# Second expert layer with W2 stationary and 512 tokens moving, with the relu's result multiplied by the choice on GpSimd

## The chip, the cores and the metric

The kernel runs on one core of a Trainium2 chip. The metric is the device time of one execution, in microseconds. The core has five engines that run side by side and hand work over by semaphores: TensorE (PE, matmuls, results in the PSUM banks), VectorE (DVE), ScalarE (ACT), GpSimd (POOL) and SyncE (SP), which issues most of the DMAs. Each engine takes its instructions strictly in the order of its own list.

## The reference

Two attentions and a mixture of experts over x of shape (2, 1024, 128), all in float32.

```
x = layernorm(x + attention_1(x))                 # 8 heads of 16, causal
x = x + attention_2(rmsnorm(x) * norm1_w)         # 16 heads of 8, through a latent of 64, causal
h = rmsnorm(x) * norm2_w
top = argmax(h @ gate_w.T + gate_b)               # one of 4 experts for each token
y_e = relu(h @ W1[e].T + b1[e]) @ W2[e].T + b2[e] # 128 -> 512 -> 128, all 4 experts
x = layernorm(x + sum_e onehot(top)[e] * y_e)
```

Every expert is computed for every token, and the choice (0 or 1) selects one of the four results.

## The kernel before

Tokens are split into batches b (0, 1) and blocks i (0, 1) of 512 tokens, each four tiles of 128. The attentions are worked off in 12 groups of four heads: groups 0 to 3 are the first attention, 4 to 7 the second attention of batch 0, 8 to 11 that of batch 1. A group needs its row maxima first (matmuls in `maxima`, L1137 to L1148, reduced on DVE by L1552), then scores (L1169), the exponential on ACT (L1338), on diagonal steps a mask on POOL (`mask`, L1044), the product with the values (`weigh`, L1186), a copy out of PSUM (L1343) and a transpose (`turn`, L1197).

Between these the program places the smaller stages. `ready(b, i)` makes the input of the experts: feed, y, residual (L1582), square, the inverse root in 13 short DVE steps on [128, 4] (`inverse_root`, L1474 to L1490), hat and x12 on POOL (L1095, L1101), feed and feat once more, gate (L1251) and `pick` (L1519 to L1527), which makes `onehot`. `experts(b, i)` is the stage that is changed. It has 16 chunks c of 128 hidden units, four to an expert e:

- `hidden` (L1318): one matmul with a chunk of W1 stationary and the block's 512 tokens of `feat` moving, into a bank of its own.
- `relu` (L1400): ACT reads that bank, adds b1 and writes `hid`, which holds two experts' chunks.
- `expert` (L1255 to L1264): when all four chunks of expert e are there, for each of the four token tiles t one small bf16 matmul for b2 (L1260) and four matmuls (L1262) with the tile's 128 tokens of `hid` stationary and 128 columns of W2 moving. A float32 matmul stands in the trace as two matmul instructions, so a tile has eight rows of L1262.
- `pick_up` (L1649): four DVE instructions an expert, each `xn = psum * onehot[e] + xn` for 128 tokens.

After the last expert of a block come the moments, the inverse root, the layer norm and the store.

The order of all instructions is made ahead of time by `order`: each step has a wanted position in units of groups (`EXPERTS`, `READY`, ...), a cost in `COSTS` and a list of steps it needs, and the planner always takes the step with the smallest sum of expected stall and position. `EXPERTS` puts the blocks of batch 0 at 7.9 to 11.4, so beside the attention of groups 8 to 11, and those of batch 1 at 11.6 to 14, mostly behind the last group, which ends with group 12. Banks for the small stages come from a pool: while the attention runs, only banks 2 and 3 (`SIDE`) are in it; after the step `quiet`, all eight. A bank is given out again when the reader named in `READER` has read it; `expert` holds one bank for one expert, from its first tile to its `pick_up`.

## Time and profile before

| | |
|---|---|
| median of three runs | 650.6 us |
| lowest and highest | 646.08 and 653.72 us |
| the profiled execution | 650.81 us |
| its span, first to last instruction | 649.1 us |
| busy: PE, DVE, ACT, POOL | 569.2, 427.3, 337.1, 157.4 us |
| mean granted TensorE clock | 0.95 |

The span is 1.7 us shorter than the time of the same execution. Groups 8 to 10 take about 393 to 535 us, with the experts of batch 0 beside them (hidden from 386.5 on); group 11 ends with its copy at 579.3 us, and from there to 640.4 us only the expert stages of batch 1 are left. The rest is the last block's norm and store. "Busy" for PE is the union of instructions whose ends are modelled, so full stretches mean that PE always had something under way.

### The profile page before, as it was taken

To read this page: it belongs to the slowest core of one execution; us is meant where nothing else is said; L and a number is where in the kernel's file an instruction comes from. 1 tells how busy PE (TensorE), PEld (TensorE's weight loads), DVE (VectorE), ACT (ScalarE), POOL (GpSimd) and SP (SyncE) were. 2 spreads that over 40 slices of the span, in tenths; PEclk is the share of its full clock that TensorE was granted. 3 is DMA by queue.
4 is the path that set the end of the run, shared out by engine and by line. 5 is a ranking of instruction groups with operands and counts; after the bars stand their busy time and mean duration, and the time that the engine had idled before them with its cause. 6 is when DMAs were issued, how large, how long until landed. Compare 5 with 4: busy or idle time off the path is not lost.

```text
span 649.1 us, 10791 instructions
## 1 busy us (share of the span) xinstructions
PE 569.2 (88%) x3917; PEld 262.7 (40%) x3933; DVE 427.3 (66%) x1091; ACT 337.1 (52%) x641; POOL 157.4 (24%) x213
## 2 busy tenths in 40 slices
PE   6678399878699978888999999999999998899994
PEld 3333133433233333332333344555534544357662
DVE  4589288889978785886888786856686614314313
ACT  4313165646446645754776767455575566652330
POOL 9611021325523243523121221301201102201000
PEclk9879599989889996996999999999999999899998
DMA  4966203001011002011010101001000000000000
GB/s 126 208 158 225 63 2 95 5 25 48 29 43 44 15 5 71 26 46 56 2 50 3 51 2 50 1 4 50 1 18 1 2 3 17 0 1 1 18 0 16
DMA packets 27845, 25.63 MB, mean 39 GB/s; under 512 B 7377, under 2 KB 24401, under 8 KB 27538
## 3 DMA queue, kind: packets, MB, share of 16 engines
q1 hardware_dynamic: 27410, 24.17, 13.2%
q0 software_dynamic: 384, 0.79, 0.6%
q8 instruction: 31, 0.51, 0.3%
q14 instruction: 20, 0.16, 0.1%
HBM read 17.30 MB, written 7.34 MB: 38 GB/s over the span
## 4 chain that ended last, share of the span: by engine, by line
PE 67%; DVE 9%; SPq 9%; ACT 7%; DMA 4%; issue 3%; POOL 1%; DVEq 0%; ACTq 0%
PE ps L1186 15%; PE ps L1169 11%; PE ps L1262 11%; PE ps L1318 9%; PE ps L1148 8%; ACT pr L1338 6%; SPq L889 4%; PE ps L1251 3%; PE ps L1245 2%; DVE mparts L1552 2%; PE ps L1197 2%; PE ps L1260 2%; DMA scr0k<-parts 2%; PE ps L1226 1%; PE ps L1143 1%
## 5 line engine op out<-in xcount | busy, mean ns | idle before, releaser
L1338 ACT ACTIVATE pr<-ps 128x512 f32<-128x512 f32 (+1 forms) x480 | 249.2, 555 | 194.9 <-PE ps L1169 157.3
L1552 DVE TENSOR_REDUCE mparts<-ps 128x1 f32<-128x512 f32 (+3 forms) x480 | 277.2, 629 | 91.3 <-PE ps L1148 90.1
L1148 PE MATMUL ps<-ks,qs 61*128 61x512 bf16 (+7 forms) x576 | 147.7, 341 | 17.5 <-DMA qs<-nparts 12.6
L1169 PE MATMUL ps<-qs,ks 64*128 64x512 bf16 (+7 forms) x560 | 141.6, 337 | 19.8 <-ACT pr L1338 10.3
L1186 PE MATMUL ps<-pr,vs 128*32 128x512 f32 (+3 forms) x1152 | 125.9, 509 | 6.8 <-ACT pr L1338 4.7
L1044 POOL TENSOR_SCALAR_AFFINE_SELECT pr<-pr 128x512 f32<-128x512 f32 x96 | 61.3, 639 | 282.1 <-ACT pr L1338 281.9
L1169 PEld LDWEIGHTS ps<-qs,ks 64*128 64x128 bf16 (+1 forms) x576 | 41.8, 95 | 139.7 <-ACT pr L1338 88.5
L1262 PE MATMUL ps<-w,work 128*128 128x128 f32 x512 | 74.1, 288 | 0.0
L1318 PE MATMUL ps<-feat,w 128*128 128x512 f32 x128 | 66.3, 622 | 0.1
L1148 PEld LDWEIGHTS ps<-ks,qs 61*128 61x128 bf16 (+1 forms) x576 | 49.3, 98 | 37.1 <-DVE mparts L1552 18.6
L1262 PEld LDWEIGHTS ps<-w,work 128*128 128x128 f32 x512 | 61.9, 191 | 4.3
L1400 ACT ACTIVATE work<-ps,b 128x512 f32<-128x512 f32 x64 | 43.8, 687 | 37.3 <-PE ps L1318 36.7
L1649 DVE SCALAR_TENSOR_TENSOR xn<-ps,onehot,xn 128x128 f32<-128x128 f32 x48 | 13.5, 343 | 42.1 <-PE ps L1262 42.1
L1186 PEld LDWEIGHTS ps<-pr,vs 128*32 128x32 f32 x1152 | 23.2, 108 | 44.4 <-issue 22.0
L1137 PE MATMUL ps<-cmask,identb 128*128 128x128 bf16 (+1 forms) x96 | 24.5, 256 | 7.7 <-DMA ks<-scr0k 4.0
L1318 PEld LDWEIGHTS ps<-feat,w 128*128 128x128 f32 x128 | 20.6, 189 | 19.8 <-issue 15.6
L1143 PE MATMUL ps<-cmask,identb 64*128 64x128 bf16 (+1 forms) x96 | 23.4, 244 | 0.9 <-DVE mparts L1552 0.6
L1143 PE MATMUL ps<-cmaskx,identx 64*128 64x128 bf16 (+1 forms) x96 | 23.4, 244 | 0.5 <-DVE mparts L1552 0.4
L1137 PEld LDWEIGHTS ps<-cmask,identb 128*128 128x128 bf16 x96 | 9.6, 101 | 29.1 <-DVE mparts L1552 20.6
L1145 PE MATMUL ps<-cmaskx,identx 64*128 64x64 bf16 (+1 forms) x96 | 19.3, 201 | 0.0
L1145 PE MATMUL ps<-cmask,identb 64*128 64x64 bf16 (+1 forms) x96 | 19.2, 200 | 0.0
L1343 ACT COPY ot<-ps 128x512 f32<-128x512 f32 x24 | 14.1, 587 | 7.5 <-PE ps L1186 7.5
(136 smaller groups left out, 499.6 us busy)
## 6 DMA issues: line engine op xcount, KB each, us to landing
qs<-scr0q SPq DMA_DIRECT2D x48, 64.0 KB, 4.0
qs<-scr1q SPq DMA_DIRECT2D x84, 32.0 KB
ks<-scr1k SPq DMA_DIRECT2D x84, 32.0 KB
ks<-scr0k SPq DMA_DIRECT2D x36, 64.0 KB, 2.2
scr0q<-parts SPq DMA_DIRECT2D x4, 384.0 KB, 3.0
scr0k<-parts SPq DMA_DIRECT2D x4, 384.0 KB, 4.3
scr1q<-parts SPq DMA_DIRECT2D x4, 384.0 KB, 2.5
scr1k<-parts SPq DMA_DIRECT2D x4, 384.0 KB, 2.5
```

Source lines behind the costliest of these rows:

```text
L1044: pool.affine_select(out=p, in_=p, compare_op=ALU.is_ge, fill=0.0, base=0, pattern=[[0, HG], [1, P]], channel_multiplier=-1).then_inc(done ...
L1137: pe.matmul(bank[:, :, w - P:w], identb[:, :], cmask[:, 0:nh, :], start=True, stop=False, skip_group_check=True)
L1143: pe.matmul(bank[:, :, w - P:w], low[0][own, :], low[1][own, 0:nh, :], start=True, stop=False, skip_group_check=True)
L1145: pe.matmul(bank[:, :, w - HALF:w], high[0][own, :], high[1][own, 0:nh, HALF:P], start=False, stop=False, skip_group_check=True)
L1148: last = pe.matmul(bank[:, h, :], queries(F, 0, h0 + h, i * P, P), keys(F, 0, h0 + h, 512 * c, w), start=not diagonal, stop=True, skip_gro ...
L1169: last = pe.matmul(to[:, h, :], keys(F, 3, h0 + h, j * P, P), queries(F, 3, h0 + h, qb * 512 + lo, n), start=True, stop=True)
L1186: last = pe.matmul(ps[VW * h:VW * (h + 1), PVB, lo:lo + n], vs[:, F % VSLOTS, j, VW * h:VW * (h + 1)], pr[:, st % PSLOTS, h, 0:n], start=( ...
L1262: last = pe.matmul(to, hid[:, e % 2, c, t * P:(t + 1) * P], w2[:, e * HC + c, :], start=False, stop=(c == HC - 1), skip_group_check=True)
L1318: pe.matmul(side(*step), w1[:, c * P:(c + 1) * P], feat[:, columns(b, i)], start=True, stop=True).then_inc(done["hidden"], 1)
L1338: act.activation(pr[:, st % PSLOTS, h0:h0 + nh, 0:STEPS[st][3]], scores_at(F, v), ACT.Exp, scale=GROUPS[F][0].scale).then_inc(exped, 1)
L1400: act.activation(hid[:, c // HC % 2, c % HC, :], side("hidden", b, i, c), ACT.Relu, bias=b1[:, c:c + 1]).then_inc(done["relu"], 1)
L1552: dve.tensor_reduce(mparts[:, F % SLOTS, h0:h0 + nh, i, c], maxes_at(F, u), AX_X, ALU.max).then_inc(taken, 1)
```

## The change

The second layer is turned round. `expert(b, i, c)` now works by chunk: W2's chunk is stationary, the 512 tokens of `hid` move, and all 16 chunks of a block are summed in one bank. So that the sum over experts is the mixture, each chunk of `hid` is multiplied in place by 0 or 1 before (`picked`, on GpSimd). The factor is needed with tokens along the free dimension and the same in all partitions. `choice_turn` (PE) and `choice_copy` (ACT) turn the choice round, `spread` (PE) and `spread_copy` (ACT) repeat one expert's row in 128 partitions, four times a block, into `masks`. b2 is added by one matmul with the choice moving. The sum, 128 features by 512 tokens, is copied out by ACT (`mix`), turned back by four transposes (`mix_turn`), and one DVE addition (`pick_up`) adds it to the residual. `masks`, `chosen` and `yT` lie in memory that earlier stages have left. The bank of the sum is held from a block's chunk 0 to its `mix`.

The plan's own figures are 0.9 for an `expert` chunk, 1.2 for `picked`, 0.35 for `choice_turn`, 0.23 for `spread`, 0.6 for the three copies, 0.58 for `mix_turn` and 0.7 for `pick_up`; positions in `EXPERTS` stay.

```diff
 def experts(b, i):
 
-    out = []
-    for c in range(E * HC + 2):
-        if c < E * HC:
-            out += [("hidden", b, i, c), ("relu", b, i, c)]
-        if c % HC == 1 and c > HC:
-            e = c // HC - 1
-            out += [("expert", b, i, e, t) for t in range(4)] + [("pick_up", b, i, e)]
-    return out + [("moments", 2, b, i)] + root("result", b, (i,)) + [("layer_norm", 2, b, i), ("out", b, i)]
+    chunks = range(E * HC)
+    return ([("choice_turn", b, i), ("choice_copy", b, i)]
+            + [(kind, b, i, e) for e in range(E) for kind in ("spread", "spread_copy")]
+            + [(kind, b, i, c) for c in chunks for kind in ("hidden", "relu", "picked", "expert")]
+            + [("mix", b, i), ("mix_turn", b, i), ("pick_up", b, i), ("moments", 2, b, i)]
+            + root("result", b, (i,)) + [("layer_norm", 2, b, i), ("out", b, i)])
 
 
 READER = {"feed": "feat", "y": "residual", "latent": "lat_copy", "lat_turn": "lat_feat", "v_proj": "v_out",
-          "gate": "pick", "hidden": "relu", "expert": "pick_up"}
+          "gate": "pick", "choice_turn": "choice_copy", "spread": "spread_copy", "hidden": "relu", "expert": "mix",
+          "mix_turn": "pick_up"}
 
...
-    if kind == "relu":
-        b, i, c = a
-        turn = 4 * (2 * b + i) + c // HC - 2
-        return [("hidden", *a)] + [("expert", turn // 8, turn // 4 % 2, turn % 4, 3)] * (turn >= 0)
-    if kind == "expert":
-        return [("relu", *a[:2], a[2] * HC + HC - 1), ("b2_parts",)]
+    if kind in ("relu", "picked", "expert"):
+        own = {"relu": "hidden", "picked": "relu", "expert": "picked"}[kind]
+        before = E * HC * (2 * a[0] + a[1]) + a[2] - 2 * HC
+        return ([(own, *a)] + [("spread_copy", *a[:2], a[2] // HC)] * (kind == "picked")
+                + [("expert", before // (2 * E * HC), before // (E * HC) % 2, before % (E * HC))] * (kind == "relu" and before >= 0)
+                + [("choice_copy", *a[:2]), ("b2_parts",)] * (kind == "expert"))
+    if kind == "choice_turn":
+        return [("pick", *a), ("lo", 15)]
+    if kind == "choice_copy":
+        return [("choice_turn", *a)]
+    if kind == "spread":
+        return [("choice_copy", *a[:2])]
+    if kind == "spread_copy":
+        return [("spread", *a)] + [("picked", 0, a[1], a[2] * HC + HC - 1)] * (a[0] == 1)
+    if kind == "mix":
+        return [("expert", *a, E * HC - 1)] + [("mix_turn", 0, a[1])] * (a[0] == 1)
+    if kind == "mix_turn":
+        return [("mix", *a)]
     if kind == "pick_up":
-        return [("expert", *a, 3), ("pick", *a[:2]), ("x12", *a[:2])]
+        return [("mix_turn", *a), ("x12", *a)]
...
-                    bank_reader[bank] = (READER[kind],) + step[1:4]
+                    bank_reader[bank] = (READER[kind],) + (step[1:3] if kind == "expert" else step[1:4])
...
-        b2p = sb("b2p", [3, E * C], BF16)
-        ones3 = sb("ones3", [3, P], BF16)
+        b2p = sb("b2p", [PARTS * E, C], BF16)
+        own_row = sb("own_row", [PARTS * E, E, P], BF16)
...
+        masks = parts[:, :, :, :].rearrange("p s a n -> p (s a) n")
+        chosen = cos[0:PARTS * E, :].bitcast(BF16)
+        yT = vall[:, 0:T].rearrange("p (i n) -> p i n", i=2)
...
-            pool.memset(ones3[:, :], 1.0).then_inc(made, 1)
+            pool.memset(own_row[:, :, :], 0.0).then_inc(gchain, 1)
+            pool.wait_ge(gchain, 4)
+            pool.affine_select(out=own_row[:, :, :], in_=own_row[:, :, :], compare_op=ALU.not_equal, fill=1.0,
+                               base=0, pattern=[[-1, E], [0, P]], channel_multiplier=1).then_inc(made, 1)
...
+                elif kind == "picked":
+                    b, i, c = args
+                    pool.wait_ge(done["spread_copy"], nth("spread_copy", b, i, c // HC))
+                    pool.wait_ge(done["relu"], nth("relu", b, i, c))
+                    pool.tensor_tensor(hid[:, c // HC % 2, c % HC, :], hid[:, c // HC % 2, c % HC, :],
+                                       masks[:, E * i + c // HC, :], ALU.mult).then_inc(done["picked"], 1)
...
-            def expert(b, i, e, t):
-
-                to = side("expert", b, i, e, t)[:, t * P:(t + 1) * P]
-                wait_bank("expert", b, i, e, t)
-                pe.wait_ge(done["relu"], nth("relu", b, i, e * HC + HC - 1))
-                pe.matmul(to, ones3[0:3, :], b2p[0:3, e * C:(e + 1) * C], start=True, stop=False, skip_group_check=True)
-                for c in range(HC):
-                    last = pe.matmul(to, hid[:, e % 2, c, t * P:(t + 1) * P], w2[:, e * HC + c, :],
-                                     start=False, stop=(c == HC - 1), skip_group_check=True)
-                last.then_inc(done["expert"], 1)
+            def expert(b, i, c):
+
+                to = side("expert", b, i, c)
+                wait_bank("expert", b, i, c)
+                if c == 0:
+                    pe.wait_ge(b2_moved, 16 * 3)
+                    pe.wait_ge(done["choice_copy"], nth("choice_copy", b, i))
+                    pe.matmul(to, b2p[:, :], chosen[:, columns(b, i)], start=True, stop=False, skip_group_check=True)
+                pe.wait_ge(done["picked"], nth("picked", b, i, c))
+                pe.matmul(to, w2[:, c, :], hid[:, c // HC % 2, c % HC, :], start=False, stop=(c == E * HC - 1),
+                          skip_group_check=True).then_inc(done["expert"], 1)
...
+                elif kind == "choice_turn":
+                    b, i = args
+                    pe.wait_ge(done["pick"], nth("pick", b, i))
+                    wait_bank(*step)
+                    for t in range(4):
+                        last = pe.matmul(side(*step)[0:PARTS * E, t * P:(t + 1) * P],
+                                         choice[:, TB * b + 4 * i + t, :, :].rearrange("p a e -> p (a e)"), identb[:, :],
+                                         start=True, stop=True)
+                    last.then_inc(done["choice_turn"], 1)
+                elif kind == "spread":
+                    b, i, e = args
+                    pe.wait_ge(done["choice_copy"], nth("choice_copy", b, i))
+                    wait_bank(*step)
+                    pe.matmul(side(*step), own_row[:, e, :], chosen[:, columns(b, i)],
+                              start=True, stop=True).then_inc(done["spread"], 1)
+                elif kind == "mix_turn":
+                    b, i = args
+                    pe.wait_ge(done["mix"], nth("mix", b, i))
+                    wait_bank(*step)
+                    for t in range(4):
+                        last = pe.transpose(side(*step)[:, t * P:(t + 1) * P], yT[:, i, t * P:(t + 1) * P], ident[:, :])
+                    last.then_inc(done["mix_turn"], 1)
...
-                    if c % HC == 0 and nth("expert", b, i, c // HC, 3) > 8:
-                        act.wait_ge(done["expert"], nth("expert", b, i, c // HC, 3) - 8)
+                    if nth("expert", b, i, c) > 2 * HC:
+                        act.wait_ge(done["expert"], nth("expert", b, i, c) - 2 * HC)
                     act.wait_ge(done["hidden"], nth("hidden", b, i, c))
                     act.activation(hid[:, c // HC % 2, c % HC, :], side("hidden", b, i, c), ACT.Relu,
                                    bias=b1[:, c:c + 1]).then_inc(done["relu"], 1)
+                elif kind == "choice_copy":
+                    b, i = args
+                    if (b, i) == (0, 0):
+                        act.wait_ge(done["lo"], nth("lo", 15))
+                    act.wait_ge(done["choice_turn"], nth("choice_turn", b, i))
+                    act.copy(chosen[:, columns(b, i)], side("choice_turn", b, i)[0:PARTS * E, :]).then_inc(done["choice_copy"], 1)
+                elif kind == "spread_copy":
+                    b, i, e = args
+                    if (b, i, e) == (0, 0, 0):
+                        act.wait_ge(b2_moved, 16 * 3)
+                        for M in range(16 - PARTS, 16):
+                            act.wait_ge(stored[M % PARTS], stored_value(M))
+                    if b == 1:
+                        act.wait_ge(done["picked"], nth("picked", 0, i, e * HC + HC - 1))
+                    act.wait_ge(done["spread"], nth("spread", b, i, e))
+                    act.copy(masks[:, E * i + e, :], side("spread", b, i, e)).then_inc(done["spread_copy"], 1)
+                elif kind == "mix":
+                    b, i = args
+                    if b == 1:
+                        act.wait_ge(done["mix_turn"], nth("mix_turn", 0, i))
+                    act.wait_ge(done["copy_v"], nth("copy_v", ATT[0].groups + ATT[1].gb - 1))
+                    act.wait_ge(done["expert"], nth("expert", b, i, E * HC - 1))
+                    act.copy(yT[:, i, :], side("expert", b, i, E * HC - 1)).then_inc(done["mix"], 1)
...
-                dve.engine_nop().then_inc(done["pick"], 1)
+                dve.tensor_copy(choice[:, t, :, :], onehot[:, t, :].unsqueeze(2).broadcast_to([P, 4, PARTS, E])).then_inc(done["pick"], 1)
...
-                    b, i, e = args
-                    dve.wait_ge(done["expert"], nth("expert", b, i, e, 3))
-                    if e == 0:
-                        dve.wait_ge(done["x12"], nth("x12", b, i))
-                    else:
-                        dve.wait_ge(done["pick_up"], nth("pick_up", b, i, e - 1))
-                    for t in range(TB * b + 4 * i, TB * b + 4 * i + 4):
-                        last = dve.scalar_tensor_tensor(out=xn[:, t, :], in0=side("expert", b, i, e, 0)[:, (t % 4) * C:(t % 4 + 1) * C],
-                                                        scalar=onehot[:, t, e:e + 1], in1=(xn if e else x0)[:, t, :],
-                                                        op0=ALU.mult, op1=ALU.add)
-                    last.then_inc(done["pick_up"], 1)
+                    b, i = args
+                    dve.wait_ge(done["x12"], nth("x12", b, i))
+                    dve.wait_ge(done["mix_turn"], nth("mix_turn", b, i))
+                    dve.tensor_tensor(tiles(xn, b, i), tiles(x0, b, i), side("mix_turn", b, i).rearrange("p (t c) -> p t c", c=C),
+                                      ALU.add).then_inc(done["pick_up"], 1)
...
```

## Rows read from the trace of the kernel before

**Rows 1.** The page's busy time, share of the span and instruction count of each engine.

```profile
PE 569.2 (88%) x3917; PEld 262.7 (40%) x3933; DVE 427.3 (66%) x1091; ACT 337.1 (52%) x641; POOL 157.4 (24%) x213
```

**Rows 2.** The page's chain that ended last, shares by engine.

```profile
PE 67%; DVE 9%; SPq 9%; ACT 7%; DMA 4%; issue 3%; POOL 1%; DVEq 0%; ACTq 0%
```

**Rows 3.** Stretches: length, busy PE, PEld, DVE, ACT, POOL, clock, DMA share, GB/s.

```profile
330.00:360.00 30.00, 28.26 (x254) 10.62 (x252) 25.55 (x51) 21.48 (x43) 5.53 (x9) 1.00 0.11 29
393.00:445.00 52.00, 51.17 (x390) 25.75 (x386) 33.92 (x82) 29.80 (x58) 7.78 (x11) 1.00 0.07 18
535.00:580.00 45.00, 41.38 (x260) 19.09 (x260) 13.40 (x59) 26.46 (x52) 7.43 (x10) 0.96 0.02 7
580.00:640.40 60.40, 59.30 (x329) 40.79 (x328) 16.46 (x74) 18.87 (x28) 2.31 (x2) 1.00 0.02 5
```

**Rows 4.** The page's groups of instructions: busy us, mean ns, then idle before.

```profile
L1044 POOL TENSOR_SCALAR_AFFINE_SELECT pr<-pr 128x512 f32<-128x512 f32 x96 | 61.3, 639 | 282.1 <-ACT pr L1338 281.9
L1262 PE MATMUL ps<-w,work 128*128 128x128 f32 x512 | 74.1, 288 | 0.0
L1649 DVE SCALAR_TENSOR_TENSOR xn<-ps,onehot,xn 128x128 f32<-128x128 f32 x48 | 13.5, 343 | 42.1 <-PE ps L1262 42.1
L1343 ACT COPY ot<-ps 128x512 f32<-128x512 f32 x24 | 14.1, 587 | 7.5 <-PE ps L1186 7.5
```

**Rows 5.** Chain of waits, 577 to 611 us: start, length, what.

```profile
577.36 0.86 PE ps L1318 x2
579.21 1.05 PE ps L1318 x2
580.27 0.44 PE ps L1197 x4
593.02 0.97 PE ps L1251 x8
594.15 1.09 PE ps L1262 x8
595.39 1.09 PE ps L1262 x8
606.60 4.29 PE ps L1318 x10
```

**Rows 6.** Timeline of PE, 85 to 93 us: start, length, instruction.

```profile
86.53 0.38 PE L1169 MATMUL ps<-qs,ks 128*128 128x512 bf16 x1
86.75 0.38 PE L1148 MATMUL ps<-ks,qs 125*128 125x512 bf16 x1
```

**Rows 7.** Timeline of DVE and POOL, 585 to 593 us.

```profile
585.45 0.69 DVE L1582 TENSOR_TENSOR x<-x,ps 128x512 f32<-128x512 f32 x1 [4.12 <-PE ps L1251]
589.98 1.04 POOL L1095 TENSOR_TENSOR xn<-x,rstd 128x512 f32<-128x512 f32 x1 [29.87 <-DVE rstd L1490]
```

**Rows 8.** Groups of POOL instructions, shapes kept apart: busy us, mean ns, idle before.

```profile
L1074 POOL TENSOR_TENSOR work<-work,parts 128x512 f32<-128x512 f32 x8 | 9.3, 1156 | 10.4 <-ACT parts L1363 10.3
```

**Rows 9.** Chain of waits, 634 to 642 us.

```profile
634.47 0.70 ACT work L1400
640.38 1.14 DVE xn L1649 x4
```

**Rows 10.** Timelines of POOL and PE in the first 26 us.

```profile
2.13 0.40 POOL L976 TENSOR_SCALAR_AFFINE_SELECT cmask<-cmask 128x256 bf16<-128x256 bf16 x1
25.44 0.37 PE L1137 MATMUL ps<-cmask,identb 128*128 128x256 bf16 x1 [4.03 <-DMA ks<-scr0k]
```

**Rows 11.** Timeline, 130 to 136 us, POOL and DVE.

```profile
132.24 0.15 DVE L1488 SCALAR_TENSOR_TENSOR rstd<-rstd 128x4 f32<-128x4 f32 x1
132.41 1.27 POOL L1069 TENSOR_TENSOR work<-work 128x512 f32<-128x512 f32 x1 [3.65 <-DVE work L1635]
132.42 1.27 DVE L1489 TENSOR_TENSOR rstd<-rstd 128x4 f32<-128x4 f32 x1
```

**Rows 12.** Groups of instructions between 400 and 560 us: the product with the values.

```profile
L1186 PE MATMUL ps<-pr,vs 128*32 128x512 f32 (+3 forms) x352 | 37.2, 494 | 1.4 <-ACT pr L1338 0.9 <-POOL pr L1044 0.4
```

More of the change, by code:

```diff
@@ L266 @@
 EXPERTS = [[(7.9, 9.7), (9.7, 11.4)], [(11.6, 13.0), (13.0, 14.0)]]
-OWN_LANE = {"evac": "out of banks", "turn": "out of banks", "combine": "row maxima", "turnmax": "row maxima",
+OWN_LANE = {"expert": "mixture", "mix": "mixture", "choice_turn": "choice", "choice_copy": "choice", "evac": "out of banks", "turn": "out of banks", "combine": "row maxima", "turnmax": "row maxima",
             "rows": "row maxima", "proj": "projections", "rotate": "projections", "rotated": "projections",
             "v_proj": "values", "v_out": "values"}
-OWN_LANE |= {kind: kind for kind in ("hidden", "relu", "expert", "pick_up", "x1", "x12", "scores", "pv", "mask", "copy_v", "quiet",
+OWN_LANE |= {kind: kind for kind in ("hidden", "relu", "picked", "spread", "spread_copy", "x1", "x12", "scores", "pv", "mask", "copy_v", "quiet",
                                      "pads", "ones", "halves", "weights", "b2_parts", "partners")}
@@ L585, in order @@
         if kind in READER or kind == "proj":
-            if not (kind == "expert" and step[4]):
+            if not (kind == "expert" and step[3]):
                 bank = choose(shared)
```

27 lines of the change are left out of this document (15 added, 12 removed).

## The prediction

> **What bounds the kernel now.** I read the page's busy shares first: PE is at 88% and nothing else comes near it [rows 1]. The chain that ended last gives PE 67%, DVE and the SP queue 9% each [rows 2]. Then the stretches, because the change touches only the part behind 386 us. With the experts of batch 0 beside the attention PE is busy 51.17 of 52.00 us, behind group 11 it is 59.30 of 60.40; at 330 to 360, attention alone, it is 28.26 of 30.00 and DVE is at 25.55 [rows 3]. The granted clock in the loaded stretches is 1.00, which is 2.4 GHz, so no term below has a part for the clock. Only group 11, 535 to 580, has some room: 3.6 us of PE idle. So from 393 us on the length is the sum of PE's work; what is taken off PE comes off the time, as long as no new wait opens a gap.
>
> **What is removed from PE.** A unit is one expert's tile: a bias matmul and eight passes of L1262. Two units in a row start 1.24 us apart, 1.09 of it the passes [rows 5]. There are 512/8 = 64 units [rows 4]: 64 x 1.24 = 79.4 us, half beside attention, half at the end.
>
> **What is added to PE.** An expert chunk has the form of `hidden`: float32, 128x128 stationary, 512 moving. Ten passes of that form take 4.29 us, 0.429 each [rows 5]; two passes a chunk, 64 chunks: 54.9 us. Why it is cheaper for the same number of columns: eight gate passes that move 4 columns take 0.97 us, hardly less than the 1.09 of eight that move 128 [rows 5]. So about 0.12 us of a short pass is its weight load, which a 512-column pass covers. The four b2 matmuls and sixteen spreads are bf16 with 512 columns; two such in a row start 0.22 us apart [rows 6]: 20 x 0.22 = 4.4, from 3.2 (at 0.16, the bias matmul's share of a unit) to 7.6 (at 0.38, one alone). Sixteen small matmuls of `choice_turn`: 0.12 each like a gate pass, 1.9, from 1 to 2.5. Four `mix_turn` at the 0.44 of a `turn` [rows 5]: 1.8. Sum added 63.0 us, net 79.4 - 63.0 = **16.4 us less**, between 12 and 18 by these bounds.
>
> **The other engines.** DVE loses 64 instructions of 0.343, 22 us [rows 4], and gets four additions at 0.69 [rows 7]; it was off the path beside PE, so I count nothing, and a gain of a few us is a bound below. ACT gets 16 spread copies, 4 choice copies and 4 `mix` at 0.587 [rows 4]: 14.1 us, hidden in stretches where it was busy 29.80 of 52.00 and 18.87 of 60.40; without that cover the 14.1 would stand in front of exponentials. POOL gets 64 products of 128x512 with one float32 and one bf16 source at 1.156, the nearest row [rows 8]: 74 us on an engine busy 157. Per chunk that is 1.16 beside 1.72 of PE (hidden plus expert), so POOL keeps pace. SP gets no new DMA; the three b2 moves only change shape.
>
> **What of it lies on the path.**
> - The end of the last block. Before, PE's last tile is followed by `pick_up`, 1.14 [rows 9]. Now `mix` 0.59, four transposes 0.44, the addition 0.69 and some 0.3 of hand-overs: +1.0 (0.6 to 1.5).
> - The last chunk must pass relu (0.70, [rows 9]) and product (1.16) before its matmul; two earlier expert chunks, 1.72, cover most of that. Before, relu alone was waited for at this place. Difference 0, between -0.5 and +1.
> - Start-up. POOL's constants grow by a memset and a select on 512 columns. The select on 256 took 0.40, and PE's first maxima waited 4.03 us for K data whose loads are in part issued by POOL behind those constants [rows 10]. +0.5, from 0 to 1.3.
> - Exposed waits. When PE comes to a matmul whose input is not there, its weight load shows: the same two passes cost 1.05 instead of 0.86 [rows 5]. Hiddens and experts now alternate with PSUM and POOL hand-overs between them. One in eight of 64 chunks at 0.19: 1.5, from 0 to all of them, 12.
> - The chain to block (1,1). Its input (residual, 13 short DVE steps, hat, feed) is made while PE works on block (1,0). The trace shows what POOL does to such steps: a DVE step on 4 columns took 1.27 us, exactly as long as the POOL product that began 0.01 before it, and its neighbour 0.15 [rows 11]. POOL now multiplies two thirds of the time there. Nine of the 13 steps read two SBUF operands, six more do in `pick`, at worst 15 x 1.1 = 16 us. Cover: at that point about ten chunks of (1,0), 17 us, and then the hiddens of (1,1), 14 us. I charge 1.5, from 0 to 6.
>
> The Trainium skill, SBUF — State Buffer, section "Who interferes with whom", says that a DVE instruction with two SBUF inputs contends with a GpSimd instruction that reads SBUF, and that whoever comes later is blocked for the whole instruction. The trace agrees, with the 1.27.
>
> **Sum.** 650.8 (the profiled execution: span 649.1 and 1.7 around it) - 16.4 + 1.0 + 0.5 + 1.5 + 1.5 = 638.9, say **639 us**. The profiled execution is 0.2 above the median of the three runs, so this holds against the median too: 1.8% less.
>
> **The rivals.**
> 1. *One side bank.* While attention runs only two banks serve the small stages, and the sum now keeps one for nearly a whole block; every hidden, spread, feed and gate shares the other. A hidden then waits for the relu of the one before: 0.17 + 0.70 after 0.86. For it: some 40 chunks lie ahead of `quiet`. Against: there are 4 to 5 us of other work per chunk, and the planner knows the bank. It is also the way in which the change would not do what it says: if the planner can't place the cheaper work, the saved PE time stands there as idle. If a third of 40 leave 0.87 open, 11.6 us: 639 + 11.6 = 650.5, no change. Chance 0.15.
> 2. *POOL holds the masks.* Slower than before. POOL is in order; a mask (0.64) can stand behind a product (1.16) that runs, or one that still waits for its relu. PE's product with the values waits for the mask, and ACT can't write `pr` ahead of it for more than four steps. Place: groups 8 to 11, 8 masks each, 32 of the 96 [rows 4]. Price: if half the masks have a running product and the relu's 0.17 in front and it reaches PE, 0.75 a mask, 24 us: 639 + 24 = 663. It decides from (650.8 - 638.9)/32 = 0.37 us a mask (0.58 for 1% slower). Against: between 400 and 560 us only 0.4 of PE's idle before that product was put down to POOL [rows 12], and PE has other work. Chance 0.15.
> 3. *POOL's grip on the short DVE steps* at block (1,1), or POOL pacing the end (16 x 1.16 where PE needs 16 x 0.86): the 6 of the bound in place of 1.5, and 1.5 more at the end: 645. Chance 0.06.
> 4. *Columns alone set the price.* Were a pass of 128 columns a quarter of one of 512, 0.107, the old units would cost 8 x 0.107 + 0.15 = 1.0 each, 64.4 in all, and 1.4 would be saved: 650.8 - 1.4 + 4.5 = 653.9. The rows show the old passes directly at 0.136, and a 4-column pass at 0.121, so it keeps a chance of 0.02.
>
> The Trainium skill states such a rule, in TensorE: Matmul & The Clock Gate, section "Back-to-back issue gap": an isolated gap is the columns over 2.4 GHz plus 2.5 ns. The same section says that for small column counts it leaves out the weight load, and the trace agrees with that half, with 0.136 where columns give 0.107.
>
> **How the numbers follow.** The forecast case, all terms inside their bounds, has 0.62; its own range is 631 to 645. Below: net 18 saved, no exposed wait, a few us from DVE. The range that holds 8 in 10 runs from 630, with 0.05 under it, through cases 1, 3 and 4, to 656, with 0.13 of case 2 above. About 1%, 6.5 us, can be told from no change. Faster by more, under 644.1: the 0.62. Within: cases 1, 3 and 4, 0.23. Slower by more: case 2, 0.15.
>
> **What would show it.** After the change: 64 expert chunks at two passes of about 0.43 back to back; `picked` 1.16 each; from the copy of group 11 (579.3 now) to PE's end 53 us rather than 61; the copy itself 7 to 8 us earlier; PE still over 95% busy from 393 us on. Rival 1 would show as PE idle released by relu in groups 8 to 10, rival 2 as L1186 waiting on POOL's mask for over 10 us, rival 3 as L1488 to L1490 over 1 us in the last 70 us. The forecast is wrong if group 8 to 10 take as long as before, or if PE stands open behind 580.

## The result: 1.1% slower, and the profile after

| | before | after |
|---|---|---|
| median of 16 runs | 649.4 us | 656.4 us |
| lowest and highest | 644.56 and 653.72 | 651.13 and 661.55 |
| span of the profiled execution | 649.1 us | 652.6 us |

The ratio is 1.0112, with a 95% interval from 1.0083 to 1.0142. The forecast was 639.

The busy line of the page after, which answers to [rows 1]:

```profile
PE 567.7 (87%) x3521; PEld 223.1 (34%) x3537; DVE 422.8 (65%) x1035; ACT 349.8 (54%) x665; POOL 231.5 (35%) x278
```

PE has 396 instructions fewer and almost the same busy time. The page's groups of the new second layer, with the hidden layer (L1346) beside it and the product with the values (L1213):

```profile
L1213 PE MATMUL ps<-pr,vs 128*32 128x512 f32 (+3 forms) x1152 | 128.5, 519 | 7.9 <-ACT pr L1388 5.1
L1127 POOL TENSOR_TENSOR work<-work,parts 128x512 f32<-128x512 f32 x64 | 73.6, 1158 | 100.6 <-ACT work L1450 86.4
L1291 PE MATMUL ps<-work,w 128*128 128x512 f32 x128 | 68.3, 624 | 1.3 <-POOL work L1127 1.2
L1346 PE MATMUL ps<-feat,w 128*128 128x512 f32 x128 | 67.2, 619 | 1.3 <-ACT work L1450 0.8
L1291 PEld LDWEIGHTS ps<-work,w 128*128 128x128 f32 x128 | 21.1, 188 | 28.4 <-POOL work L1127 14.5
```

Two things were as foreseen: the product takes 1.158 us (1.156 forecast), and PE hardly stands for it, 1.2 us in all. But the weight loads of the chunks stood 14.5 us for the product; a load that comes late is not covered (two such passes take 1.05 us with an open load and 0.86 in a row, [rows 5]), and the page doesn't count that as idle time of the matmuls.

**Where the time is.** The stretch that the change touches runs from the first hidden matmul to the last matmul of the second layer. Its row before and its row after, each from a view of stretches (length, then busy PE, PEld, DVE, ACT, POOL, clock, DMA share, GB/s), the first one from the kernel before:

```profile
386.50:640.35 253.85, 246.74 (x1680) 130.02 (x1679) 123.68 (x360) 132.23 (x247) 28.49 (x41) 0.99 0.04 11
```

```profile
386.20:642.81 256.61, 242.87 (x1264) 89.03 (x1263) 118.13 (x297) 143.33 (x268) 101.62 (x105) 0.97 0.04 10
```

PE is busy 3.9 us less, but the stretch is 2.8 us longer: PE now stands 13.7 us in it and not 7.1. And the clock is lower. Cut into pieces, after:

```profile
390.00:393.90 3.90, 3.80 (x23) 1.36 (x20) 3.68 (x8) 3.81 (x9) 2.12 (x3) 1.00 0.33 97
393.90:397.30 3.40, 3.40 (x18) 1.26 (x17) 1.39 (x3) 1.53 (x4) 0.01 (x1) 0.51 0.34 95
397.30:400.70 3.40, 3.40 (x24) 1.98 (x22) 1.62 (x3) 1.04 (x2) 0.64 (x1) 0.99 0.00 0
475.80:479.20 3.40, 3.40 (x16) 0.49 (x15) 1.89 (x4) 0.98 (x2) 0.00 (x0) 0.51 0.14 40
550.60:557.40 6.80, 6.33 (x32) 1.93 (x32) 1.57 (x6) 3.19 (x8) 1.27 (x2) 0.53 0.12 39
```

and the one such place before:

```profile
557.40:560.80 3.40, 3.40 (x16) 1.02 (x8) 0.20 (x2) 1.14 (x4) 2.31 (x2) 0.50 0.00 0
```

The granted clock falls to half, 1.2 GHz, for 3.4 us at a time, which costs 1.7 us of full-speed work: 6.8 us after, 1.7 before. So PE's work at full clock is 242.9 - 6.8 = 236.1 against 246.7 - 1.7 = 245.0: **8.9 us less**, where the forecast was 16.4. The whole account of the two profiled spans: first hidden -0.3, work -8.9, clock +5.1, idle +6.6, behind the last matmul +1.0 (9.8 for 8.8): +3.5 = 652.6 - 649.1. The loss to the clock is an estimate throughout, the length of a stretch times one minus its granted clock.

The medians differ by 7.0; the profiled execution lies 1.4 above the median before, and 2.0 below it after. The timed executions tell what the profiled ones leave out, since each lists its span and its mean granted clock. Over those that the ratio counts, span times (1 - clock) is 38.7 us after, at a mean clock of 0.941, and 31.1 for the kernel before, at 0.952 (25 executions timed with e1 to e4, median 647.6 us). Span times clock, an estimate of what would be left without slow clock, is 615.6 after and 614.6 before. So in the timed executions most of the difference goes with the clock, and apart from the clock the change saved nothing.

Two places of the chain that ended last show new waits. At the input of block (1,1):

```profile
590.44 0.64 ACT feat L1431
591.10 0.70 DVE rstd L1683
591.83 1.16 DVE rstd L1547
593.01 1.09 DVE rstd L1557
594.12 1.09 DVE rstd L1558
597.05 1.05 POOL xn L1116
```

L1547, L1557 and L1558 work on four columns. The three steps at this place in the chain of the last block, where no product runs, take 0.18 us each; here they take 1.1, together +2.8 us. What POOL did at the time, from its timeline:

```profile
591.79 3.38 POOL L1127 TENSOR_TENSOR work<-work,parts 128x512 f32<-128x512 f32 x3 [4.18 <-ACT work L1450]
```

The Trainium skill, SBUF — State Buffer, section "Who interferes with whom", has whoever comes later blocked for the whole instruction; the trace agrees, with 1.09 to 1.16 beside three products that take 3.38 together. The nine steps behind them took 0.17 each, since no product ran then. Of the 2.8 us, 1.4 reached PE as idle time, from 596.7 on. At the end:

```profile
637.57 0.87 PE ps L1346 x2
638.52 0.70 ACT work L1450
639.36 1.17 POOL work L1127
640.56 2.25 PE ps L1291 x4
642.91 0.59 ACT vall L1474
643.64 0.64 PE ps L1370 x4
644.38 0.70 DVE xn L1718
```

From the end of the last hidden matmul to the next of the second layer 2.1 us pass (638.44 to 640.56); before it was 0.86, and no chunk was left to put in between. "ps L1346" is the hidden layer and "ps L1291" the second.

### The profile page after: what moved, and what is told of

Same layout as the page of the kernel before. It is cut to its first block, busy times and chain, and to the rows that moved or that the text cites. A ratio compares the mean times of both kernels' runs of the same rounds, so it can differ in the third digit from the quotient of the medians.

```text
span 652.6 us, 10153 instructions
## 1 busy us (share of the span) xinstructions
PE 567.7 (87%) x3521; PEld 223.1 (34%) x3537; DVE 422.8 (65%) x1035; ACT 349.8 (54%) x665; POOL 231.5 (35%) x278
## 4 chain that ended last, share of the span: by engine, by line
PE 63%; DVE 10%; SPq 9%; ACT 9%; DMA 4%; issue 4%; POOL 2%; DVEq 0%; ACTq 0%; POOLq 0%
PE ps L1213 15%; PE ps L1196 11%; PE ps L1291 9%; PE ps L1346 8%; PE ps L1175 8%; ACT pr L1388 6%; SPq L907 4%; PE ps L1278 3%; PE ps L1272 2%; DVE mparts L1625 2%; SPq L958 2%; PE ps L1253 2%; PE ps L1224 2%; DMA scr0k<-parts 1%; PE ps L1170 1%
## 5 line engine op out<-in xcount | busy, mean ns | idle before, releaser
L1213 PE MATMUL ps<-pr,vs 128*32 128x512 f32 (+3 forms) x1152 | 128.5, 519 | 7.9 <-ACT pr L1388 5.1
L1127 POOL TENSOR_TENSOR work<-work,parts 128x512 f32<-128x512 f32 x64 | 73.6, 1158 | 100.6 <-ACT work L1450 86.4
L1291 PE MATMUL ps<-work,w 128*128 128x512 f32 x128 | 68.3, 624 | 1.3 <-POOL work L1127 1.2
L1346 PE MATMUL ps<-feat,w 128*128 128x512 f32 x128 | 67.2, 619 | 1.3 <-ACT work L1450 0.8
L1213 PEld LDWEIGHTS ps<-pr,vs 128*32 128x32 f32 x1152 | 23.5, 109 | 50.9 <-issue 24.4
L1291 PEld LDWEIGHTS ps<-work,w 128*128 128x128 f32 x128 | 21.1, 188 | 28.4 <-POOL work L1127 14.5
L1346 PEld LDWEIGHTS ps<-feat,w 128*128 128x128 f32 x128 | 21.1, 189 | 22.1 <-issue 17.8
L1718 DVE TENSOR_TENSOR xn<-x,ps 128x512 f32<-128x512 f32 x4 | 2.7, 686 | 36.2 <-PE ps L1370 36.2
L1522 DVE RECIPROCAL rc<-ps 128x16 f32<-128x16 f32 x24 | 6.0, 251 | 29.7 <-PE ps L1224 29.5
L1090 POOL TENSOR_TENSOR work<-work 128x512 f32<-128x512 f32 x8 | 10.2, 1270 | 31.2 <-DVE work L1708 31.2
L1164 PEld LDWEIGHTS ps<-cmask,identb 128*128 128x128 bf16 x96 | 9.6, 101 | 31.1 <-DVE mparts L1625 20.3
```

The source lines that it names most:

```text
L1127: pool.tensor_tensor(hid[:, c // HC % 2, c % HC, :], hid[:, c // HC % 2, c % HC, :], masks[:, E * i + c // HC, :], ALU.mult).then_inc(done ...
L1164: pe.matmul(bank[:, :, w - P:w], identb[:, :], cmask[:, 0:nh, :], start=True, stop=False, skip_group_check=True)
L1213: last = pe.matmul(ps[VW * h:VW * (h + 1), PVB, lo:lo + n], vs[:, F % VSLOTS, j, VW * h:VW * (h + 1)], pr[:, st % PSLOTS, h, 0:n], start=( ...
L1291: pe.matmul(to, w2[:, c, :], hid[:, c // HC % 2, c % HC, :], start=False, stop=(c == E * HC - 1), skip_group_check=True).then_inc(done["ex ...
L1346: pe.matmul(side(*step), w1[:, c * P:(c + 1) * P], feat[:, columns(b, i)], start=True, stop=True).then_inc(done["hidden"], 1)
```

## The experiments

Three explanations were tested first: the one side bank (rival 1), the choosing with its product, and chunks that stand alone with an open weight load (a weight load that no other matmul covers). A fourth, the new order of everything, came out of them.

All ratios are to the kernel before, run on the same chip. The chips differ between groups of runs, and e3, e4, e5, e8 and e9 compute something else than the reference, which their texts say. For each kernel the same stretch is read as above, from its first hidden matmul to its last of the second layer, in us:

| | ratio, 95% interval | length | PE busy | idle | lost to clock | busy at full clock |
|---|---|---|---|---|---|---|
| before | 1 | 253.9 | 246.7 | 7.1 | 1.7 | 245.0 |
| after | 1.0112 [1.0083, 1.0142] | 256.6 | 242.9 | 13.7 | 6.8 | 236.1 |
| e9, the form in the old order, no b2 | 0.9790 [0.9750, 0.9830] | 235.7 | 227.5 | 8.3 | 0 | 227.5 |
| e3, no choice | 0.9976 [0.9943, 1.0009] | 250.9 | 238.1 | 12.8 | 1.7 | 236.4 |
| e8, no choice, four sums | 1.0004 [0.9983, 1.0026] | 251.9 | 239.5 | 12.4 | 1.7 | 237.8 |
| e4, short product | 1.0121 [1.0065, 1.0176] | 252.4 | 241.3 | 11.1 | 6.8 | 234.5 |
| e13, after, places x | 1.0055 [1.0025, 1.0084] | 251.8 | 238.4 | 13.3 | 0 | 238.4 |
| e15, after, places y | 1.0087 [1.0048, 1.0126] | 251.2 | 240.0 | 11.2 | 3.4 | 236.6 |
| e10, after, replanned | 0.9955 [0.9914, 0.9997] | 243.8 | 235.6 | 8.2 | 0 | 235.6 |
| e14, before, places x | 1.0055 [1.0017, 1.0092] | 256.3 | 248.4 | 8.0 | 3.4 | 245.0 |
| e16, before, places y | 1.0058 [1.0035, 1.0081] | 252.5 | 246.6 | 5.9 | 1.7 | 244.9 |
| e11, before, replanned | 0.9969 [0.9936, 1.0002] | 251.2 | 245.0 | 6.1 | 0 | 245.0 |
| e17, end's product on DVE | 0.9885 [0.9844, 0.9925] | 241.8 | 234.9 | 6.9 | 0 | 234.9 |

The last column is the control of the reading: four orders of the kernel before give 244.9 to 245.0, five of the changed one (e17 among them) 234.9 to 238.4. Within one kernel the order moves the idle time and the clock, much less the work. The rows are those of one execution each, and it isn't always a typical one: e15's was 6.7 us faster than its median, e17's 4.6, e10's 3.0.

**Was it the one bank, held to the end of the attention (rival 1)?** The step `quiet`, which opens all banks, was moved forward, in the changed kernel and in the one before.

```diff
-                 ... (NF + 0.9, ("quiet",))])
+                 ... (NF + 0.02, ("quiet",))])
```

> The changed kernel with one number altered: `quiet`, the step after which all eight banks are open to the small stages, stands at position 12.02 instead of 12.9, right behind group 11. Theory A (the sum's bank starves the end: between the copy of group 11 at 576.4 us and `quiet` each hidden has one bank and waits for the relu of the one before): the end gets 3 to 5 us shorter, about 652 us. Theory B (the time is lost by matmuls of the experts that stand alone among attention work and show their weight load) and theory C (the choosing itself, its product and copies, holds PE up) expect no change, 656.

> The kernel before with `quiet` at 12.02. Before, an expert gives its bank back after its pick_up, so both side banks are in use. Theory A expects under 1 us here, so 649; if it gains as much as the changed kernel does, the early release is a gain of its own and says nothing on the sum's bank.

Measured 653.4 us, 1.0067 [1.0027, 1.0107], and 1.0025 [0.9998, 1.0051]. The 653.4 lies between the two forecasts. But the changed kernel's end, from the last copy of group 11 on, was no shorter (67.1 us for 66.4), and of what the timed executions gained, 2.9 us is clock (span times (1 - clock) 35.8 for 38.7) and 1.5 the rest (614.1 for 615.6). So the bank at the end isn't it.

**What does the choosing cost?** e3 leaves out the choice: no `choice_turn`, `spread`, copies or product; every chunk goes into the sum as it is.

```diff
-            + [(kind, b, i, e) for e in range(E) for kind in ("spread", "spread_copy")]
-            + [(kind, b, i, c) for c in chunks for kind in ("hidden", "relu", "picked", "expert")]
+    return ([(kind, b, i, c) for c in chunks for kind in ("hidden", "relu", "expert")]
```

> The changed kernel without choosing: choice_turn, choice_copy, spread, spread_copy and picked are left out, and the output is the sum over all four experts (b2 comes in with a constant). W2 stationary, 512 tokens moving, one bank for the sum, `mix` and the turn back stay. Theory C (choosing): most of the 16 us that TensorE saves plus the chain of 4 to 5 us before block (1,0) come back, 638 to 641 us. Theories A and B (bank, lone matmuls): only the work of choosing goes, 6 us of TensorE, so about 649 to 651.

Measured 645.6 us. Without the choosing the kernel is faster by 1.4% of the kernel before (1.0112 - 0.9976), some 9 us, and still wins nearly nothing. The 9 us are not the price of choosing as work: e3 has a new order too, and by the table it lost 5.1 us less to the clock, while its busy time at full clock is the same, 236.4 for 236.1. Over the timed executions span times (1 - clock) is 30.3 for 38.7, and span times clock 613.8 for 615.6.

**The product's length.** e4 multiplies 8 of the 512 columns, with the same order as the changed kernel.

```diff
-  pool.tensor_tensor(hid[:, c // HC % 2, c % HC, :], hid[...], masks[:, E * i + c // HC, :], ALU.mult)
+  pool.tensor_tensor(hid[:, c // HC % 2, c % HC, 0:8], hid[...], masks[:, E * i + c // HC, 0:8], ALU.mult)
```

> The changed kernel, same plan, with the GpSimd product on 8 of the 512 columns (the rest of the hidden layer isn't multiplied): all waits stay, the product takes 0.1 to 0.2 us instead of 1.16. If the product's length is what holds TensorE and the masks up, 4 to 8 us faster, 649 to 652; theories A and B expect 1 us or less, the short steps of VectorE that were held by the product (1.1 to 1.2 us each) included: 655.

```profile
L1127 POOL TENSOR_TENSOR work<-work,parts 128x8 f32<-128x8 f32 x64 | 12.9, 202 | 143.2 <-ACT work L1450 129.0
```

POOL lost 61 us of work and the time stayed, 1.0121 with four executions. That doesn't make the product free. In the profiled execution the stretch is 4.2 us shorter, and in the timed ones span times clock is 4.3 us less (611.3 for 615.6); the clock took it back, 0.937 on average for 0.941, 41.5 us lost for 38.7. So the length of the product costs about 4 us, by this estimate. Of rival 2 nothing is left: the matmuls of the attention take as long as with the full product, 109.1 us for 109.2 from start to start.

**Is it PE's columns at all?** e5 moves 256 of 512 columns in each chunk of the second layer.

```diff
-  pe.matmul(to, w2[:, c, :], hid[:, c // HC % 2, c % HC, :], ...
+  pe.matmul(to[:, 0:256], w2[:, c, :], hid[:, c // HC % 2, c % HC, 0:256], ...
```

> The changed kernel, same plan, with each expert matmul moving 256 of the 512 tokens (the other half of the sum is left out): 0.43 us less of TensorE per chunk, 27.5 in all, 12 of it in groups 8 to 10. Theory D (in groups 8 to 10 TensorE's work fills waits for the exponential and the maxima, so that the number of pieces sets the pace and not their length): the three groups shrink by under 5 us, the end by its 13, about 640. If TensorE's sum of work sets the length there, 12 and 13: about 630.

Measured 637.1 us, 0.983 [0.9772, 0.9888]: 2.8% or 18 us less than the changed kernel, of the 27 that PE's columns lose (half of 54.9). That lies between the two forecasts. PE's work does set the length for the most part, but about a third of what is taken off comes back as idle time (18.0 us in the stretch for 13.7) and clock (10.2 for 6.8).

**Is it the lone chunk, whose weight load nothing covers?** A lone chunk costs 1.02 us and one in a row 0.86 (of the 64 after, 41 take 1.01 on average to the next start, 17 take 0.86). e6 and e7 run chunks in twos and in fours, with the plan's cost of a run to match.

```diff
+                for k in range(c - RUN + 1, c + 1):
+                    last = pe.matmul(to, w2[:, k, :], hid[:, k // HC % 2, k % HC, :], ...)
```

> The changed kernel with two chunks' expert matmuls issued as one run, planned anew. Theory B (a lone chunk costs 1.02 instead of 0.86 because its weight load shows): half of the loads are covered, 64 x 0.08 = 5 us less, 651. Theory D: fewer pieces to fill the waits with, so nothing or some us more, 656 to 658.

> The changed kernel with an expert's four chunks as one run of 3.4 us, planned anew. Theory B: 64 x 0.12 = 8 us less, 648 to 650. Theory D: a run of 3.4 us is longer than the waits it fills and keeps the attention's next matmuls back, 656 or more.

Measured 653.0 us, 1.0091 [1.0046, 1.0137], between its two forecasts, and 657.7, 1.0135 [1.0079, 1.0191], where theory D had it. From start to start the chunks of e7 take 59.8 us and not 64.3, so loads are covered; but its clock loses 13.6 us and its hidden matmuls take 6 us more. Nothing is won. Both have an order of their own, so they don't price the cover alone.

**Four sums in place of one.** e8 is e3 with a bank for each expert again and a DVE addition each.

```diff
+    ... for kind in ("hidden", "relu", "expert", "mix") if kind != "mix" or c % HC == HC - 1]
```

> The kernel without choosing (the sum over all four experts is the output) and with the bank given back after every expert: VectorE copies or adds 128x512 into yT four times a block instead of one copy on ScalarE. Against the kernel without choosing that keeps one bank (0.998 of the kernel before). Theory A (the bank that the sum keeps slows hiddens and feeds) expects 5 to 8 us less than that, 0.987 or below; theories B and D expect no difference beyond 2 us.

Measured 1.0004 [0.9983, 1.0026], no better than e3. It isn't quite a clean test: four sums need four b2 matmuls a block in place of one, which is 3.7 us more from start to start in the stretch, and the whole stretch is only 1.0 longer. So the long-held bank may cost some 3 us; the 5 to 8 of theory A, and the 11.6 of rival 1, it doesn't.

**The form alone, in the old order.** e9 is the kernel before with each expert's four tiles replaced by its four chunks, same steps, same places; b2 is left out, and `pick_up` reads its bank as before.

```diff
-                pe.matmul(to, ones3[0:3, :], b2p[0:3, e * C:(e + 1) * C], start=True, stop=False, ...)
-                for c in range(HC):
-                    last = pe.matmul(to, hid[:, e % 2, c, t * P:(t + 1) * P], w2[:, e * HC + c, :], ...)
+                last = pe.matmul(to, w2[:, c, :], hid[:, e % 2, t, :], start=(t == 0), stop=(t == HC - 1), ...)
```

> The kernel before, instruction for instruction in its order, but each of the 64 expert units (bias matmul and eight passes with 128 columns) is one chunk with W2 stationary and 512 tokens moving, four of them summed in the expert's bank. b2 is left out, and pick_up reads the bank as if tokens lay in partitions, so the output is not the reference's; all waits, banks and steps of VectorE, ScalarE and GpSimd stay. If the new form's saving is real and what ate it is the new order, 64 x (1.24 - 0.86) less the lone load shown by a third of them = 18 to 22 us less, 0.966 to 0.972 of the kernel before. If the saving is eaten by the waits of the attention wherever it is made, under 10 us, 0.985 or more.

The first two lines of its page, and the stretch:

```profile
span 632.0 us, 9911 instructions
...
PE 556.5 (88%) x3485; PEld 218.3 (35%) x3485; DVE 428.5 (68%) x1091; ACT 337.3 (53%) x641; POOL 156.9 (25%) x213
```

```profile
387.60:623.31 235.71, 227.46 (x1232) 84.86 (x1231) 123.50 (x360) 132.15 (x247) 28.38 (x41) 1.00 0.04 11
```

Measured 633.2 us, 0.979, 14 us less, between the two forecasts. Not all of it is the form. In the stretch the passes of the second layer took 68.6 us before, from start to start, and the 64 b2 matmuls 9.9; e9 has 61.0 for its chunks and no b2. So of 17.5 us the chunks saved 7.6, and leaving b2 out 9.9 (the changed kernel's four b2 matmuls take 1.3).

Beside e3 (0.9976) this is the main finding: the same chunks in a newly planned order are 12 us slower. The stretch is 15.2 us longer (250.9 for 235.7). 2.9 of that are e3's b2 matmuls and turns, 2.5 its chunks (63.5), and 11.0 the matmuls of the attention. Their time from start to start, over the last 887 of them in each kernel, is 100.1 us before, 99.8 in e9, but 109.2 after and 110.8 in e3. After, little of the 9.1 us is work: busy time at full clock is 94.1 for 92.9. The rest is idle time behind these matmuls, 9.8 for 6.1, and slow clock, 5.3 for 1.2. In e3 the idle time is 12.0 and the busy time 97.6.

**Other orders.** So the order itself was varied, in both kernels alike: the places of batch 0's blocks alone (x: e13, e14; y: e15, e16), and with the plan's cost of `hidden` at 1.0 (e10, e11; e10 with the early `quiet` too).

```diff
-EXPERTS = [[(7.9, 9.7), (9.7, 11.4)], ...
+EXPERTS = [[(8.1, 9.9), (9.9, 11.6)], ...      # x
+EXPERTS = [[(7.9, 9.9), (9.9, 12.0)], ...      # y, and replanned
```

> The changed kernel with `quiet` at 12.02, a hidden entered into the plan at 1.0 (it measured 1.02 to 1.05 alone) and the two expert blocks of batch 0 wanted at 7.9 to 9.9 and 9.9 to 12. If the order is what costs in groups 8 to 10, 5 to 8 us less than the changed kernel with quiet early, 645 to 648; if the choosing and the form cost it, within 2 us of that kernel, 652.

> The kernel before with the same two alterations of its plan (hidden 1.0, batch 0 wanted at 7.9 to 9.9 and 9.9 to 12), as a control of how far a plan alone moves the time. If the old plan was a favourable one, 3 to 6 us more, 651 to 653; if the altered positions are a gain in themselves, 3 to 5 less.

> The changed kernel, only the wanted positions of batch 0's experts moved to 8.1 to 9.9 and 9.9 to 11.6. If the change costs time whatever its order (theory F), 1.00 to 1.02 of the kernel before, 647 to 660 us. If it is only that its first order was a bad one (theory O), 0.99 to 1.00, 641 to 648, and about what its partner, the kernel before with the same positions, shows, less some us.

> The kernel before with the positions 8.1 to 9.9 and 9.9 to 11.6. Theory O: the old plan isn't special, within 0.6% of the kernel before. Theory F says nothing on it.

> The changed kernel with only the positions moved to 7.9 to 9.9 and 9.9 to 12, hidden's cost and quiet as they were. Theory F: 647 or more. Theory O: near the replanned version's 0.9955, 643 to 647, which would also say that quiet and hidden's cost had no part in it.

> The kernel before with the positions 7.9 to 9.9 and 9.9 to 12, as partner of the changed kernel with the same. Theory O: 643 to 649; the changed kernel would then stand within 4 us of it on either side. Theory F: the changed kernel is over 4 us slower than it.

Changed minus before, order by order: +1.1% (the original), 0.0% (x), +0.3% (y), -0.1% (replanned, where only e10 has the early `quiet`), each difference known to about 0.5%, the first to 0.3%. e10 (643.8 us) is even faster than the first of its forecasts, e11 (645.0, 2.4 less than the kernel before) is near its second. By their own times e13 (651.1 us) and e15 (653.4) came out where theory F had them, and not theory O; only the pairs speak for O. And in no order does the new form show the 1.8% that were forecast: the new order explains the 1.1%, and not why the gain is missing in all four.

The clock goes with it in part: changed minus before, the stretch lost +5.1, -3.4, +1.7 and 0 us in the profiled executions, and span times (1 - clock) over the timed ones is +7.6, -2.3, +2.7 and +3.4. The falls come back with an order: the kernels that share the changed kernel's order in the attention (after, e1, e4, e5) all have one within 390 to 402, one within 470 to 484 and one from 550 on; e2, e9, e10, e11, e13 and e17 have none between 380 and the end of the second layer. But e6, e7 and e12, which have other orders, share the first one, and the timed executions of the changed kernel have mean clocks from 0.933 to 0.953, so the falls aren't the same in each. What PE did before: the longest spell without work in the ten us ahead of the fall at 393.9 was 0.43 us (at 384.2), ahead of that at 475.8 it was 0.18 (at 474.2). e10 has spells of 0.42 and 0.30 at 383.4 and 391.3, without a fall, so the rows don't show which of them brings it.

**Choosing on DVE.** e12 drops the product and has DVE multiply each expert's bank by its mask and add it up, in a new order.

```diff
+                        link(dve.tensor_tensor(part[:, :], bank, mask, ALU.mult))
+                        dve.tensor_tensor(yT[:, i, :], yT[:, i, :], part[:, :], ALU.add)
```

> A version without the GpSimd product: W2 stationary, 512 tokens moving, but each expert's four chunks are summed in a bank of their own and VectorE multiplies that sum by the choice (0.7 us) and adds it to yT (0.6 us), so no expert matmul waits for choice or product and every bank comes back after one expert; quiet at 12.02, hidden 1.0, batch 0 wanted at 8.1 to 9.9 and 9.9 to 11.7. TensorE's work is 2.6 us more than in the changed kernel (twelve more b2 matmuls). If choosing ahead of the matmul cost the end its 10 us, 643 to 647; if VectorE's 21 us more hold the maxima up, 650 or more.

Measured 658.4 us, 1.0196 [1.0134, 1.0258]: worse, with 12.0 us idle and 5.1 lost to the clock. It changes the order and the engine at once, so it doesn't tell which of them.

**A version that beats both.** e17 is e10 with the products of batch 1, most of which lie behind the attention, on DVE.

```diff
-                elif kind == "picked":                     # POOL
+                elif kind == "picked" and args[0] == 0:    # POOL
+                elif kind == "picked" and args[0] == 1:    # DVE, the same product
```

> As the changed kernel on its new list of places (quiet from group 12.02, a hidden unit at 1.0 us, the block (0,0) and (0,1) ending at 9.9 and 12.0; 643.8 us, 0.9955 of the kernel before), and with the products of the two blocks of batch 1, which are all but the last ones run, done on VectorE and not on GpSimd. If GpSimd's product and its hold on VectorE's short steps are a price at the end: each product 0.7 and not 1.16 us, the chain ahead of block (1,1) about 3 us shorter, the last chunk 0.5 us earlier, and VectorE has 32 products of 0.7 us among its own steps: 640 us. If VectorE's own steps (the maximum, the masks) are then held up behind the products, 644 to 648 us.

Measured 641.0 us against 648.9, 0.9885 [0.9844, 0.9925]. Two groups of its page and its end:

```profile
L1131 POOL TENSOR_TENSOR work<-work,parts 128x512 f32<-128x512 f32 x32 | 37.0, 1158 | 65.6 <-ACT work L1454 65.0
L1724 DVE TENSOR_TENSOR work<-work,parts 128x512 f32<-128x512 f32 x32 | 23.2, 748 | 21.1 <-ACT work L1454 21.1
```

```profile
608.88 2.58 PE ps L1350 x6
611.45 2.76 PE ps L1295 x6
614.22 2.58 PE ps L1350 x6
616.79 2.76 PE ps L1295 x6
619.55 2.58 PE ps L1350 x6
622.12 2.78 PE ps L1295 x6
```

The product takes 0.748 and not 1.158, and hidden and chunks come in sixes, back to back to the end. From group 11's copy to the end of the matmuls it takes 60.9 us (564.0 to 624.9), in the changed kernel 66.4. But e10 is the kernel to compare with, and there it is 62.8 already. From e10 to e17 the stretch is 2.0 us shorter (243.8 and 241.8), and another 2.3 lies ahead of the first hidden matmul (385.4 and 383.1), where no product runs. The planner knew the product's new engine and cost, so the order behind the attention changed too; the two effects are not separated. That e17 beats the kernel before is measured; what of it the engine did is not.

## Why the prediction was wrong

**Three things in the sum failed: the price of a chunk, the waits of which it had one in eight, and the attention, which it took to stay as it is.** Time from the start of each matmul to the start of the next adds up to the stretch and counts idle time and slow clock with the matmul ahead of them:

| us from start to start | before | after | forecast for after |
|---|---|---|---|
| second layer with b2 | 78.5 | 65.6 | 55.8 |
| choosing and turning back | 0 | 9.3 | 7.2 |
| hidden | 63.9 | 61.8 | no change |
| attention | 101.7 | 109.2 | no change |
| feeds and gate | 9.7 | 10.8 | no change |
| sum, the stretch | 253.9 | 256.6 | |

(The stretch after holds 16 of the attention's matmuls fewer, 887 for 903.)

Step by step, as the sum had them:

- *Removed minus added, -16.4.* By the first two lines it is 78.5 - 65.6 - 9.3 = 3.6 us less. The 78.5 is what the sum had for the removed part (79.4). The part that failed most is the chunks: 64 x 0.858 = 54.9 is the price back to back, and they took 64.3, 1.00 each. Without idle time and slow clock they are still 62.2, 0.97 each, and even in e9, in the old order, 61.0. The choosing and b2 are 10.6, forecast 8.1.
- *Exposed waits, +1.5.* This term was mis-sized: "one in eight of 64 chunks". 45 of the 64 chunks took over 0.95 us to the next start, so the dear chunk was the rule and not the exception. The 9.4 us over 54.9 lie inside the bound of 12 that the same sentence gave. Of them 1.9 is idle time and 0.3 slow clock.
- *The attention left as it is, 0.* No term stood for it, and without its 7.5 us the result would have been some 4 us faster and not slower. The planner puts all steps in a new order when the list changes. What grew is mostly idle time (+3.7) and slow clock (+4.1). The clock fell three times in the stretch (once for double length) and not once. The prediction read the clock in the old order, 1.00, and took it as given for the new one.
- *The end, +1.0.* Right: 9.8 for 8.8 behind the last matmul, though its own terms add up to 0.9. *The last chunk, 0 between -0.5 and +1:* 1.3 measured, just outside. *Start-up, +0.5:* not seen, the first hidden matmul is 0.3 earlier.
- *The chain to (1,1), +1.5, from 0 to 6.* Right in size, 1.4 us of PE idle from 2.8 in three steps, but it counted other steps: the nine with two SBUF operands, which ran at 0.17. The three that stood beside products have one tensor operand each.

By busy time at full clock the same miss reads: 8.9 us less and not 16.4, 6.6 more idle time where the sum had 3.0 for waits, and 5.1 for a clock that had no term.

**The signs.** "53 us rather than 61" from group 11's copy: it was 66.4. The copy came 2.9 us earlier (576.4 for 579.3) and not 7 to 8. PE was busy 94.6% of the stretch. "If group 8 to 10 take as long as before" was named as the mark of a wrong forecast, and it came: 146.5 us after, 141.7 before.

**The rivals.** 1: refuted at its price of 11.6 us by e1 and e8, though the time fell beyond its 650.5; some 3 us of it stay possible. 2: the result lies towards it, for another reason; PE waited for POOL's masks 1.0 us (0.4 before) and not 24 (idle before the product with the values, 386.2 to 577 us, by line):

```profile
L1213 PE MATMUL ps<-pr,vs 128*32 128x512 f32 (+3 forms) x392 | 45.0, 533 | 2.5 <-ACT pr L1388 1.4 <-POOL pr L1065 1.0
```

3: its grip is real, and by e4 the length of the product costs about 4 us; moving it to DVE at the end goes with 0.7% between e10 and e17, which ran on two chips and whose intervals overlap. 4: its 653.9 is near the measured time, by chance: the old passes took 68.6 us and not the 54.8 that columns alone give, and the chunks were cheaper in every order, 7.6 us in e9 and 4.3 after.

**What stays open.** Which property of an order leaves PE idle between the attention's matmuls and lets the clock fall; the orders of e10 and e17 are without both (5.4 us idle there, no fall), but what sets them apart was not isolated. Nor is it shown why a chunk costs 0.97 with no idle time counted: the open weight load is the likely cause, and e7, with chunks in fours, has 57.1 for all 64, but in another order.

## What to carry to other kernels

Where a planner orders everything, a changed step changes everything: rows of the old order price the work, not the waits or the clock, and here the order alone was worth from -0.3% to +0.6% for the old kernel and from -1.6% to 0 for the new. Test the new form in the old order first (e9), to know what it is worth, and count what such a test leaves out; then look for an order for it, and compare it with the old form in as many orders. Compare the granted clock of the timed executions as well: a change of 4 us (e4) was hidden behind it. And price a matmul that waits for another engine with its weight load, unless the trace shows such matmuls in rows.

## What the runs showed of the hardware

- The granted clock fell to 1.2 GHz for 3.4 us, or 6.8, once right behind 3.9 us in which PE was busy 3.80; and four kernels with the same order had falls in the same three spans.
- Three DVE steps on four columns with one tensor operand each took 1.09 to 1.16 us beside POOL products, and 0.18 alone.
- The same product of 128x512 in place takes 0.748 us on DVE and 1.158 on POOL; a POOL product of 8 columns takes 0.202.
